# V of the next expert unit made at the end of the preceding section

## What is computed

```
x = x + _L0_attn_ref(_layernorm(x, axis=-1), ...)   # causal attention, 16 heads of 16
x = x + _L0_ffn_ref(_layernorm(x, axis=-1), ...)    # experts that are attentions
x = x + _L1_attn_ref(_layernorm(x, axis=-1), ...)   # causal attention with rotary positions
x = x + _L1_ffn_ref(_layernorm(x, axis=-1), ...)    # 64 experts, top 8, and a shared one
```

```
for e in range(e_total):
    member = (top2 == e).any(-1)
    order = jnp.argsort((~member).astype(jnp.int32), axis=-1, stable=True)
    xg = jnp.take_along_axis(x, order[..., None], axis=1)
    q, k = (xg @ wq[e] + bq[e]), (xg @ wk[e] + bk[e])    # each reshaped to heads
    v = (xg @ wv[e] + bv[e]).reshape(b, s, h, hd)
    att = softmax(where(validg, einsum(q, k) * 0.5, -1e9))
    y = einsum(att, v) @ wo[e] + bo[e]
    out = out.at[bidx, order].add(wg[..., None] * y)
```

## Time and profile before

| what | value |
|---|---|
| runs, median (lowest, highest) | 4147.94 us (4140.35, 4152.86) |
| profiled execution, span from first to last instruction | 4157.8 us (its own total is not listed apart) |
| PE busy, share of the span | 3490.6 us, 84% |
| DVE busy | 2378.2 us, 57% |
| ACT busy | 2095.7 us, 50% |
| POOL busy | 877.4 us, 21% |
| mean granted TensorE clock | 0.912 |

### The profile page before, as it was taken

How to read it: one execution, slowest core, us unless ns; L and a number is a source line. 1 busy time by engine, 2 the same in 40 slices (tenths; PEclk the granted TensorE clock), 3 DMA queues, 4 the chain that set the end, 5 groups by cost and what they waited for, 6 DMA issues and landing times.

```text
span 4157.8 us, 57056 instructions
## 1 busy us (share of the span) xinstructions
PE 3490.6 (84%) x21573; PEld 1674.0 (40%) x21574; DVE 2378.2 (57%) x3496; ACT 2095.7 (50%) x4546; POOL 877.4 (21%) x674
## 2 busy tenths in 40 slices
PE   6999999687989899898898877766399878888795
PEld 3444444333333333333434333333144434345574
DVE  5566566465565656564565543322667787885423
ACT  2666566355666666565665544422165545563121
POOL 1141422312101010101011010111424232110474
PEclk8999999889999999999999988866699989999898
DMA  7554546222303030303213143333433232203488
GB/s 188 151 159 115 148 140 178 77 66 70 89 14 97 15 96 16 91 21 89 66 44 75 31 105 88 92 89 85 119 96 112 85 102 70 77 24 128 113 199 226
DMA packets 327185, 399.88 MB, mean 96 GB/s; under 512 B 43082, under 2 KB 295594, under 8 KB 319980
## 3 DMA queue, kind: packets, MB, share of 16 engines
q1 hardware_dynamic: 275916, 341.63, 29.7%
q0 software_dynamic: 18432, 35.67, 3.8%
q10 hardware_dynamic: 32560, 19.00, 2.0%
HBM read 230.48 MB, written 156.17 MB: 93 GB/s over the span
## 4 chain that ended last, share of the span: by engine, by line
PE 61%; DVE 19%; DMA 5%; ACT 4%; issue 4%; ACTq 2%; SPq 2%; POOL 1%; PEldq 0%; DVEq 0%; PEld 0%; POOLq 0%; another core or an unknown queue 0%
PE PSUM L850 15%; DVE M L1088 12%; PE PSUM L810 12%; PE PSUM L828 11%; PE PSUM L741 6%; PE PSUM L872 3%; PE PSUM L787 3%; PE PSUM L655 2%; ACTq L618 2%; ACT P L1027 2%; PE PSUM L858 1%; DVE best L1455 1%; DVE XR L1458 1%; PE PSUM L813 1%; PE PSUM L820 1%
## 5 line engine op out<-in xcount | busy, mean ns | idle before, releaser
L1088 DVE TENSOR_REDUCE M<-PSUM 128x1 f32<-128x896 f32 (+7 forms) x1702 | 1703.6, 1032 | 1103.6 <-PE PSUM L810 676.0
L1027 ACT ACTIVATE P<-PSUM 128x512 f32<-128x512 f32 (+2 forms) x3520 | 1580.6, 503 | 857.5 <-PE PSUM L828 548.2
L810 PE MATMUL PSUM<-KS,QS 99*128 99x512 bf16 (+3 forms) x3592 | 945.7, 346 | 283.7 <-issue 99.1
L828 PE MATMUL PSUM<-QS,KS 101*128 101x512 bf16 (+2 forms) x3520 | 1084.5, 346 | 94.5 <-ACT P L1027 57.6
L850 PE MATMUL PSUM<-P,VA 128*17 128x384 f32 (+3 forms) x7040 | 794.6, 529 | 4.7 <-ACT P L1027 4.7
L828 PEld LDWEIGHTS PSUM<-QS,KS 101*128 101x128 bf16 x3520 | 332.8, 99 | 841.9 <-ACT P L1027 463.0
L810 PEld LDWEIGHTS PSUM<-KS,QS 99*128 99x128 bf16 x3592 | 319.4, 101 | 697.6 <-DVE M L1088 292.6
L707 POOL TENSOR_TENSOR QF<-QF,PH 128x1024 f32<-128x1024 f32 (+4 forms) x94 | 154.6, 1645 | 1933.6 <-ACT PH L979 1893.0
L741 PE MATMUL PSUM<-XT,W 128*128 128x512 f32 (+2 forms) x656 | 298.7, 583 | 6.5 <-ACT P L1027 3.5
L850 PEld LDWEIGHTS PSUM<-P,VA 128*17 128x17 f32 x7040 | 137.5, 97 | 249.0 <-issue 211.0
L813 PE MATMUL PSUM<-identb,maskB 128*128 128x128 bf16 x1024 | 215.8, 226 | 0.0
(11 more groups left out here) (205 smaller groups left out, 3095.3 us busy)
## 6 DMA issues: line engine op xcount, KB each, us to landing
qk_d<-PH SPq DMA_DIRECT2D x120, 256.0 KB
xg_d<-GX SPq DMA_DIRECT2D x19, 1152.0 KB, 12.3
yg_d<-GX SPq DMA_DIRECT2D x17, 1152.0 KB, 8.1
XF<-xg_d SPq DMA_DIRECT2D x17, 1024.0 KB, 7.5
VA<-n_L_ffn_expert_gate_up_w SPq DMA_DIRECT2D x64, 256.0 KB, 3.8
QS<-qk_d SPq DMA_DIRECT2D x36, 384.0 KB, 5.9
KS<-qk_d SPq DMA_DIRECT2D x36, 384.0 KB, 6.2
qk_d<-PH SPq DMA_DIRECT2D x48, 224.0 KB
```

The lines of the kernel that those rows point to most:

```text
L810: mm = e.matmul(slot_heads(s, hb)[:, x, a:b], QS[0:KA, g, h + x, 128 * qt:128 * qt + 128], KS[0:KA, g, h + x, a:b], start=True, stop=not d ...
L828: mm = e.matmul(s[:, 0:q1 - q0], KS[0:KB, g, j, 128 * kt:128 * kt + 128], QS[0:KB, g, j, q0:q1], start=True, stop=not diag, skip_group_che ...
L1027: e.activation(P[:, m % NP, 0:q1 - q0], s[:, 0:q1 - q0], ACT.Exp, scale=ly.scale).then_inc(S["act_p"], 1)
L1088: e.tensor_reduce(m[:, qt, h:h + hb], v[:, :, 0:kn], AX.X, ALU.max).then_inc(S["dve_a"], 1)
```

## The change

V of a unit is no longer made in its own section. The section before makes it, after its last `nt`, between the tasks `yt` and `op` of its own output. The first layer's section makes V of the first unit near its end. Each V goes to buffer 0 of `VA`, which the unit section itself reads; ScalarE may write it when the last `pv` of the running unit is done. A section makes V for as many tiles as it believes the next unit has: its own size, and 8 in the first layer's section and in section 1. The wait for wv changes from a carried semaphore (`ahead_wv`) to an ordinary one (`next_wv`). The head of a section loses its `vp` tasks, and `s2`, `xt`, `qp` and `nv` get earlier planner times. In the final section the V of the `l1` section gets its time from the same new line.

```diff
@@ -199,0 +202,3 @@
+    def values(self, i):
+
+        return 0 if self.layer.name == "moe" else i % 2
@@ causal_order
+        ev += [(17.62 + 0.01 * k, ("vp", B, k // 2, k % 2)) for k in range(NT // 2)]
@@ next_layer
-    ev += [(36.0 + 1.5 * k, ("vp", 2, k // 2, k % 2)) for k in range(4)]
@@ unit_order
-    second = [(0.4 * len(layer.pairs()) + 0.3, step)]
+    second = [(0.3, step)]
...
-    ev += [(0.05 + 0.4 * k, ("vp", 1, c, h)) for k, (c, h) in enumerate(layer.pairs())]
...
-        ev += next_layer(0.4 * len(layer.pairs()) + 0.1)
+        ev += next_layer(0.1)
     else:
-        x = 62.0 if layer.first else 0.4 * len(layer.pairs()) + 0.1
+        x = 62.0 if layer.first else 0.1
...
         ev += [(t + 0.5 + 0.3 * k, ("yt", 1, c, k)) for k in range(2)]
         ev += [(t + 2.0 + 0.5 * h, ("op", 1, c, h)) for h in range(2) if layer.pair(c, h)]
+    t = max([t for t, task in ev if task[0] == "nt"] + [35.0] * layer.final)
+    ev += [(t + 0.6 + 0.55 * k, ("vp", 2, c, h)) for k, (c, h) in enumerate(coming.pairs())]
@@ attention_pe
-                par = i % 2
+                par = O.values(i)
...
-                    if moe and i == 1:
-                        w.carried("ahead_wv", 16)
+                    if O.ahead(i):
+                        w.wait_ge("next_wv", "nv", i)
@@ attention_act
-                    w.wait_ge("pe_v", "pv", i - 2, 3, ly.nch - 1, ly.nt - 1)
+                    if moe:
+                        w.wait_ge("pe_v", "pv", 1, 3, O.layer.nch - 1, O.layer.nt - 1)
+                    else:
+                        w.wait_ge("pe_v", "pv", i - 2, 3, ly.nch - 1, ly.nt - 1)
@@ attention_sp
                 elif kind == "w1":
-                    w.carried("ahead_wv", 16)
-                    w.wait_ge("pe_a", "vp", 1, *ly.pairs()[-1])
...
                 elif kind == "nv":
                     w.wait_ge("pe_a", "vp", i - 1, *O.layer.of(i - 1).pairs()[-1])
-                    e.sem_clear(S["ahead_wv"])
-                    e.dma_start(... wv of the next unit ...).then_inc(S["ahead_wv"], 16)
+                    e.dma_start(... wv of the next unit ...).then_inc(S["next_wv"], 16)
```

More of the change, by code:

```diff
@@ L37 @@
             + ["sh_rows", "sh_weights", "first_weights"] + [f"sh_res{b}" for b in range(B)])
-DMA_SEMS += ["w1_qkv", "w1_rest"]
+DMA_SEMS += ["w1_qkv", "w1_rest", "next_wv"]
 DMA_SEMS += ["mask0", "unit_counts", "unit_count", "unit_masks", "unit_zero", "first_iota"]
@@ L42 @@
              "add0", "add1", "fin", "out_st"] + [f"ye{x}_in{k}" for x in range(2) for k in range(2 * B)]
-AHEAD_SEMS = ["ahead_ld0", "ahead_ld1", "ahead_st0", "ahead_st1", "ahead_rows", "ahead_wv", "ahead_y"]
+AHEAD_SEMS = ["ahead_ld0", "ahead_ld1", "ahead_st0", "ahead_st1", "ahead_rows", "ahead_y"]
 FIRST_SEMS = ["first_rows", "first_ident", "first_qk", "first_vo", "first_rest"]
@@ L151, in raises @@
                 return [(f"ahead_st{ix[1]}", 48)]
-            if kind in ("nr", "nv", "yo"):
-                return [({"nr": "ahead_rows", "nv": "ahead_wv", "yo": "ahead_y"}[kind], 16)]
+            if kind in ("nr", "yo"):
+                return [({"nr": "ahead_rows", "yo": "ahead_y"}[kind], 16)]
         if kind == "gu":
@@ L1697, in attention_sp @@
                     w.wait_ge("pe_a", "vp", i - 1, *O.layer.of(i - 1).pairs()[-1])
-                    e.sem_clear(S["ahead_wv"])
                     e.dma_start(W[:, 2, :, :], kn_weights(d["L0_ffn_wv"][row(v["nex"]), :, :].rearrange(
-                        "o a b -> (o a) b"))).then_inc(S["ahead_wv"], 16)
+                        "o a b -> (o a) b"))).then_inc(S["next_wv"], 16)
                 elif kind == "nr":
```

## The result

| | kernel before | changed kernel |
|---|---|---|
| median of the runs (lowest, highest) | 4150.40 us (4140.35, 4159.49), 4 runs | 4216.00 us (4203.94, 4222.08), 4 runs |
| span of the profiled execution | 4157.8 us | 4220.0 us |
| mean granted TensorE clock | 0.912 | 0.906 |

The ratio is 1.0162, with a 95% interval of 1.0140 to 1.0183: the changed kernel is slower by 1.6%. A second measurement on another chip, where the kernel before takes 4167.33, gave 4233.11 and a ratio of 1.0161 (1.0139 to 1.0183).

What follows compares the result with a forecast made beforehand. The prediction took a section's end as one serial chain with PE its longest member. Ends 63.0, heads -11.1 and clock +7.7 sum to +59.6 us, on 4147.9 about 4208 us, range 4165 to 4234.

Steps and rivals of the forecast that it cites:

- Ends: Section ends: V ahead of the last output product lengthens the serial chain, little hidden in PE's gaps; +63.0 us.
- l0's end: End of the first layer's section: V delays the last add, partly hidden by SyncE's queued stores; +0.9 us.
- Small sections: Ends of 3-tile (9 to 12) and 2-tile (13 to 15) sections: V adds 11.6 and 9.0 us, partly at low clock.
- Heads: Section heads: removing V wins only 11.1 us, because ACT's seven issues and bk's landing are late next.
- Clock: Heads of sections 2 to 12: the clock rises later, slowing work behind; 0.7 each, +7.7 us, bounds 0 to 22.
- A: Heads: transfers don't hold them, ACT's issue alone does; heads win 40 us, time 4171; chance 0.16.
- B: Heads: attention behind V bounds the section, so all of V's 95.8 us is won; time 4115; chance 0.06.
- C: Tie: B in part, or V at the ends runs in PE's or the barrier's spare time; 4150; chance 0.08.
- D: Ends: V falls behind the chain, sparing only the bias add's 0.7 us at 15 ends; time 4198; chance 0.

Runs made afterwards that it cites:

- a1_nx: Changed kernel with the next weights and biases (wq, wk, bq, bk) issued by SyncE one section sooner: ratio 1.0012 to the kernel before.
- a4_fill: Changed kernel with idle PE time at the heads of sections 2 to 15 filled with useless matmuls: ratio 1.0117 to the kernel before.
- r1_after: The changed kernel again, unedited, on a third chip: 4233.1 us, ratio 1.0161 to the kernel before.
- a5_qllate: Changed kernel with SyncE's Q and K loads and mask of groups 2 and 3 issued later in sections 2 to 8: ratio 1.0107 to the kernel before.
- a3_behind: Changed kernel with the next unit's V sorted behind the last op instead of ahead of it: ratio 1.0116 to the kernel before.
- b3_nov: Kernel before without V in the unit sections, all other planner times kept: ratio 1.0037 to the kernel before.
- a7_wo_late: Changed kernel with wq, wk, bq, bk one section sooner, V behind op, and wo, bo, bv issued later by SyncE: ratio 0.9967 to the kernel before.
- a2_nov: Changed kernel without V in the unit sections, everything else kept: ratio 1.0063 to the kernel before.
- b2_mix: Kernel before with V's pairs interleaved with the first scores at the head instead of V first: ratio 1.0025 to the kernel before.

## Why the prediction was right

The mechanism held at its two main places: V ahead of op lengthens the serial end, and the head gives back little because ACT's issues and bk's landing were behind V. By its own steps:

- **Ends, forecast +63.0, measured +54.2.** Sections 2 to 8 were forecast at 35.8 and gave 34.1: the stretch from last pv to store grew by 5.1 (7 tiles, forecast 5.4) and by 4.4 (6 tiles, 4.7). The chain of reasoning, records at the high clock less the gap that they fill, was right to 0.3. l0's end gave 2.3 for 0.9. Section 1 gave 4.4 for 5.7, but its barrier grew by 4.2 (8.0 to 12.2), which was in no step. V alone doesn't set it: a1_nx and a4_fill make the same V there and have 8.7, r1_after 12.1. But in the other profiles with V there it is 11.6 to 12.4, and in the five without V 7.7 to 9.2. What varies it stays open.
- **Small sections, forecast 20.6, measured 9.2: the term that was mis-sized.** I priced V at the low clock in the ends of sections 10, 11 and 13 to 15, because those ends had run at it. They don't any more. Windows of the ends of sections 10 and 13 of the changed kernel, which answer to the earlier trace rows:

```profile
2574.05:2582.87 8.82, 6.78 (x33) 5.27 (x33) 1.71 (x4) 2.35 (x5) 0.00 (x0) 1.00 0.00 0
...
2768.39:2776.17 7.78, 4.76 (x23) 3.53 (x22) 1.19 (x3) 1.64 (x4) 0.00 (x0) 1.00 0.00 0
```

  The clock is 1.00 in both, with V between the pieces of the chain. So op itself got faster and paid for V: the stretch from last pv to store went from 8.39 to 8.82 and from 8.61 to 8.83 in sections 10 and 11 (forecast +3.6 each), and in sections 13 to 15 by -0.03, +0.64 and +0.92 (forecast +3.0 each); 3.1 of the 4.7 there are barriers. Sections 9 and 12, at the high clock before as well, grew by 1.9 where 2.2 was forecast. For 2-tile sections this is partly luck: in r1_after two of the three ends take 9.96, at a clock of about 0.7, as forecast. In the five profiles with V between yt and op (after, r1, a1, a4, a5) 8 of the 15 2-tile ends take 7.8 and 7 take 9.9 to 10.0, while all twenty 3-tile ends take 8.8. The step that failed took the clock of an idle stretch for a property of the place. But 3-tile ends without V run at either clock too (6.9 in all four in a3_behind, 9.9 in all four in b3_nov), and with V they ran at the higher one each time.
- **Heads, forecast -11.1, measured -8.4.** Sections 2 to 8: -6.8 for -4.8, and bk is named as the releaser in all seven. a5_qllate and a1_nx show that the transfers were the hold. Section 1 was forecast at 3.3 by its first exponential, which does start 5.1 sooner (8.0 to 3.0 behind the first record), but its last pv is only 0.7 earlier. Sections 9 to 12 won 0.3 for 3.0. The forecast took the landing of bk as the bound there, and it isn't: qp is at 8.6 to 8.8 in each section after, and bk lands at 7.2 in section 10. PE's timeline of section 10 shows what holds it:

```profile
2516.65 0.48 PE L815 MATMUL PSUM<-KS,QS 99*128 99x384 bf16 x2 [3.12 <-issue]
...
2521.84 0.50 PE L833 MATMUL PSUM<-QS,KS 101*128 101x384 bf16 x1 [3.88 <-ACT XT L965]
...
2525.33 1.67 PE L746 MATMUL PSUM<-XT,W 128*128 128x384 f32 x4
```

  PE waits 3.88 for ACT's first copy, behind the seven issues, and then works without a gap until qp, 3.49 us at a granted clock of 0.50. With four of the seven issues gone (a1_nx) these heads sum to 24.1, with all gone (a7_wo_late) to 17.4, in place of 34.7.
- **Clock, forecast +7.7 within 0 to 22, measured up to 17 in sections 2 to 8.** The stretch from first qp to last pv grew by 17.0 in sections 2 to 8 and 7.9 in 9 to 12. The direction was right: mean granted clock 0.83 in place of 1.00 in the second 12 us of the large sections. a4_fill, which brings it back to 1.00, prices it at 9.6 in this stretch and at 13.7 over the whole kernel, 3.5 of them in a barrier that it doesn't touch. So the clock cost some 10 to 14, and the term was low by 2 to 6. The Trainium skill ("TensorE: Matmul & The Clock Gate", section "HAM oscillation — how this bites in real kernels") tells of waits for transfers that drop the clock for the work behind them; the rows agree in kind, and the price is nearer to the middle of the range than to its upper end, 22.
- **What no step had.** Beyond the clock some 7 us of the 17.0 are left. More than half of that is a shift of the border at which I cut, and no loss: in the changed order six s1 records of a 7-tile section stand ahead of the first qp in place of ten, and eight in place of ten in a 6-tile one. So 22 records, 11 pairs, have moved behind it in sections 2 to 8; at the higher clock one pair takes about 0.38 from its start to the next task's (1265.60 to 1265.98 in the kernel before), 4.2 us in all. The heads' -6.8 holds the same 4.2 with the other sign. a2_nov and b3_nov, both without V, differ here by 18.8 (1200.0 and 1181.2), and not by this order alone: over the whole stretch the mean granted clock is 0.962 in a2_nov and 0.972 in b3_nov. No run changed the order of the tasks alone, so the rest stays open. In sections 13 to 15 first qp to last pv won 8.0, where nothing was forecast: PE's idle time there fell by 5.9, 5.2 of it waits for DVE, and the mean granted clock rose from 0.69 to 0.71; why is not settled.

By terms, measured less forecast, the misses had both signs: ends -8.8, heads +2.7, first qp to last pv +8.8 (16.5 for 7.7). That the sum, 62.2 measured for 59.6, is so near is partly their cancelling.

**The rivals.** A, ACT's issues alone: its time of 4171 would have needed qp without a wait for bk; the seven waits refute it. The kernel that it describes is a5_qllate: its heads in 2 to 8 are 18 to 20.5 shorter and the whole is 23.4 faster, where the prediction set 40 - 11 = 29 between the heads of the two. B, the attention bounds the section: refuted three times, by b3_nov (V gone for nothing, and slower), b2_mix (30.6 us of earlier exponentials for 4.6 at most) and a2_nov (no V in either place, and 26 slower than the kernel before). C, the tie, needed 50 of the 63 us hidden at the ends; they cost 54. D, V behind op, is excluded by the timeline; a3_behind measured it at -15.7, not -10.

## What to carry to other kernels

An engine's busy time at a section's head is no price: ask what runs behind it, and what is late next once it is gone. Here moving 96 us of matmuls gave 8 at the heads until the transfers and issues behind them were moved too (61 us); the same move of transfers was worth nothing while the cover stood. Work added to a serial end should go into the waits of its engine, or behind the last product where the barrier covers part of it, and not between the pieces of the chain.

## What the runs showed of the hardware that I had not expected

- Useless matmuls in an idle head made the kernel 13.7 us faster (4233.1 to 4219.5, two chips of the same speed). The granted clock in the 12 us behind section 3's first qp was 1.00, where the two profiles of the changed kernel have 0.86 and 0.83, and 9.6 of the gain stands between first qp and last pv of sections 2 to 8.
- The landing of the small bias transfer bk fell from 9.1 to 3.2 us when SyncE's Q and K loads were not beside it, with its issuer and its place unchanged.
- With work between the pieces of a serial chain the clock was 1.00 in all twenty 3-tile ends of five profiles, so that 12 records of V cost 0.2 to 0.4 us where the end had run at 0.79 to 0.80 before. In the 2-tile ends, with 8 records of V, it was so in 8 of 15.
